# Near-lag matmuls in whole pieces in the odd chunk steps, prefix matmuls in the even ones

## The reference

```
xp = (X @ Wp + bp).reshape(B, T, 4, D)
f  = (pos @ Wf + bf).reshape(T, 3, D)          # pos: sines and cosines
y  = xp[:, :, 0]
for i in range(3):
    y = causal_conv(y, f[:, i]) * xp[:, :, i + 1]   # the reference does it by FFT
x = layernorm(x + y)
x = layernorm(x + (silu(x @ wg.T) * (x @ wu.T)) @ wd.T)
```

## Time and profile before

| | us |
|---|---|
| median of 3 runs | 971.78 (971.59 to 972.85) |
| the profiled execution | 972.62 |
| its span, first to last instruction | 970.4 |
| PE busy | 876.6 |
| DVE busy | 767.4 |
| POOL busy | 645.3 |
| ACT busy | 529.7 |

### The profile page before, as it was taken

The page is one execution under the profiler, slowest core; times in us unless marked ns, Lnnn a source line. Parts: engine busy times, 40 slices in busy tenths (PEclk is TensorE's granted clock), DMA queues, the critical chain, the costliest instruction groups (busy, mean ns, idle before and its releaser), DMA issues. The chain is left out here.

```text
span 970.4 us, 21584 instructions
## 1 busy us (share of the span) xinstructions
PE 876.6 (90%) x8204; PEld 678.0 (70%) x8204; DVE 767.4 (79%) x1318; ACT 529.7 (55%) x1048; POOL 645.3 (66%) x679
## 2 busy tenths in 40 slices
PE   3999999947999999999999999954899999999994
PEld 2888888846888888888888888732456556555563
DVE  2777777735899898888889889846688898988864
ACT  2253334446788888878887667314344444444441
POOL 2555555403888898898898889862676666667642
PEclk8999999969999999999999999996999999999998
DMA  5596556488566567566667877328123224222011
GB/s 205 192 348 214 188 173 205 165 230 238 164 189 174 165 194 197 174 179 175 193 195 213 262 235 209 109 105 276 45 66 120 77 65 130 65 77 74 23 45 44
DMA packets 165788, 155.16 MB, mean 160 GB/s; under 512 B 3457, under 2 KB 151937, under 8 KB 165313
## 3 DMA queue, kind: packets, MB, share of 16 engines
q1 hardware_dynamic: 164176, 145.24, 49.3%
q10 hardware_dynamic: 1520, 8.68, 2.3%
HBM read 111.18 MB, written 42.73 MB: 159 GB/s over the span
## 5 line engine op out<-in xcount | busy, mean ns | idle before, releaser
L564 POOL TENSOR_TENSOR gz<-prod 128x512 f32<-128x512 f32 x180 | 230.4, 1280 | 88.2 <-DVE prod L507 87.0
L507 DVE TENSOR_TENSOR prod<-bank,wfx 128x1024 f32<-128x1024 f32 x180 | 219.8, 1221 | 32.5 <-ACT bank L437 30.7
L396 PE MATMUL bank<-gz,ei 128*128 128x256 f32 x720 | 186.8, 382 | 2.2 <-POOL gz L564 2.0
L149 PE MATMUL bank<-wps,xs 128*128 128x512 f32 x768 | 176.4, 392 | 5.6 <-POOL xs L250 5.6
L149 PEld LDWEIGHTS bank<-wps,xs 128*128 128x128 f32 x768 | 145.6, 190 | 36.1 <-DVE wps L218 5.7
L939 POOL TENSOR_TENSOR hl<-hf,hh 128x512 f16<-128x512 f32 x96 | 111.8, 1173 | 82.4 <-ACT hh L793 82.4
L437 ACT COPY bank<-bank 128x512 f32<-128x512 f32 x180 | 102.8, 571 | 105.4 <-PE bank L344 105.4
L250 POOL TENSOR_TENSOR xs<-xt,xs 128x256 fp32r<-128x256 f32 x128 | 93.3, 752 | 97.4 <-ACT xs L181 97.4
L574 POOL TENSOR_TENSOR y<-y,gate 128x256 f32<-128x256 f32 x192 | 143.3, 747 | 5.1 <-DVE y L518 5.1
L344 PE MATMUL bank<-yh,ef 128*128 128x256 f16 x720 | 137.6, 273 | 2.3 <-ACT bank L437 1.3
L396 PEld LDWEIGHTS bank<-gz,ei 128*128 128x128 f32 x720 | 122.8, 190 | 15.8 <-POOL gz L564 6.5
(11 more groups left out here) (77 smaller groups left out, 1960.2 us busy)
## 6 DMA issues: line engine op xcount, KB each, us to landing
toep<-filter_rows SPq DMA_DIRECT2D x48, 1024.0 KB, 7.1
gates<-staged SPq DMA_DIRECT2D x16, 1536.0 KB, 6.3
gate<-gates SPq DMA_DIRECT2D x48, 512.0 KB, 4.1
xt<-in_XT SPq DMA_DIRECT2D x16, 512.0 KB, 5.0
attn_out<-y SPq DMA_DIRECT2D x16, 512.0 KB, 5.5
ya<-attn_out SPq DMA_DIRECT2D x16, 512.0 KB, 4.6
xr<-in_X SPq DMA_DIRECT2D x16, 512.0 KB, 5.4
out_x<-oo SPq DMA_DIRECT2D x16, 512.0 KB, 3.4
```

The source lines that it names most:

```text
L149: mm = pe.matmul(bank[n % 4 * 2 + half][:, :], xs[:, n % XSS, half, hx, k, :], wps[:, hw, k, half * 512:(half + 1) * 512], start=(k == 0 a ...
L396: mm = pe.matmul(dst, ei[:, h, e0 * P:(e0 + 1) * P], gz[:, n % 3, h, :], start=False, stop=(h == 1))
L507: nc.vector.tensor_tensor(prod[:, n % 2].rearrange("p r j (c b) -> p r j c b", b=NB), b_copy[n % 2][:, :].rearrange("p (r c b) -> p r c b" ...
L564: nc.gpsimd.tensor_tensor(gz[:, n % 3], prod[:, n % 2, 0], prod[:, n % 2, 1], ALU.add).then_inc(gz_ready, 1)
```

## The change

`toeplitz` is called for both parts of a piece in its odd step 2q+1; before, part 0 was in step 2q+1 and part 1 in step 2q+2, for the last piece in step 0 of the next pass. The prefix had 4 chunks (8 matmuls) in each of steps 3 to 14 (3 chunks in steps 6, 10 and 14); it now has 8 chunks (16 matmuls) in steps 4, 8 and 12 and 7 chunks (14 matmuls) in steps 6, 10 and 14. Step 15 keeps its 15 chunks. No matmul is added or removed, and nothing changes on the other engines.

```diff
                     for k in range(NA):
                         if 0 <= u < NU and k < NE:
                             state(u, k)
-                        if k == 0 and 0 <= u < NU:
-                            toeplitz(u, NQ - 1, 1)
                         if u + 1 < NU:
                             if k % 2:
                                 toeplitz(u + 1, k // 2, 0)
-                            elif k:
-                                toeplitz(u + 1, k // 2 - 1, 1)
+                                toeplitz(u + 1, k // 2, 1)
                             if k == 3 and u + 2 < NU:
                                 pe.wait_ge(norm_sum, u + 3)
                             if k == NA - 1:
                                 prefix(u + 1, 3, range(NE))
-                            elif k >= 3:
-                                prefix(u + 1, (k - 3) // 4, range((k - 3) % 4 * 4, min((k - 3) % 4 * 4 + 4, NE)))
+                            elif k % 2 == 0 and k >= 4:
+                                prefix(u + 1, (k - 4) // 4, range(0, 8) if k % 4 == 0 else range(8, NE))
```

## The result

The changed kernel takes 978.18 us (median of 6, 977.23 to 979.65) for 971.78 before. The ratio is 1.0066, with a 95% interval of 1.0053 to 1.0079: slower by more than 0.2%, in the direction forecast. It is 2.4 us above the predicted 975.8 and just outside the range given, 974.2 to 978.0. The profiled execution took 977.95 us for 972.62, 5.33 more.

A forecast was written before the change was run, and what follows sets the result against it. Passes were taken as bound by PE's steps 3 to 15 plus DVE's chain over the join; 11 x 0.36 = 3.96 us plus 0.10 in the first pass gave 4.06, median 975.8 us (+0.42%), range 974.2 to 978.0.

The forecast's parts named there:

- The ring of two links: Each pass: PE's work from step 3's near lags to step 15's readout, then DVE's gather(14) to low(1), some 6.6 us.
- the three places named: Steps 1, 2 and 3: PE's extra 0.36 us idle per join spread over waits for evacuate, pb and low(1).
- the 0.47 us put down to `norm`: Step 1: norm taken to need 0.47 us before the next state, putting state(2) 0.14 us later than before.
- the sum: Whole program: 3.96 us for 11 passes plus 0.10 for the first pass, 4.06 us slower.
- Is link A still without a wait?: PE from step 3's near lags to step 15's readout: 0 for new waits, bounds 0 and 6.6 us.
- alternating steps open new waits: Rival: 0.1 us in each even step of steps 4 to 14, or a late step 2 copy; 978 to 982, chance 0.07.
- the forecast's 0.36 us: Step 15: 12 near-lag matmuls of piece 7 moved in from step 0 of the next pass add 0.36 us per pass.
- its sign of being wrong: DVE's chain shortens, waits for copies, combine or evacuate appear in steps 4 to 14, or the 227.28 filter load shifts.
- The first pass: Pass u = -1, bound by a filter load until 227.28: +0.10 us, bounds -0.1 and +0.2 for the work behind it.
- No net cost: Rival: DVE's chain in the join shortens with PE's work, passes keep 34.83 us; about 971.9 us, chance 0.05.
- faster: Rival: pb starts ahead of POOL's combine, saving 0.78 us in each of 10 joins; about 967.6 us, chance 0.04.
- The gain in the first pass: Rival: half the first pass's time at the lower clock goes, -1.65 us; 974.2 us, chance 0.04.

The follow-up runs named there:

- run 1: Changed kernel with part 1 of piece 7 back in step 0 of the next pass: 973.49 us, ratio 1.0008 to the kernel before.
- run 3: Kernel before the change, with only part 1 of piece 7 moved from step 0 of the next pass to step 15: 976.65 us, ratio 1.0043.
- run 4: Kernel before the change, with all of piece 7 moved to step 0 of the next pass: 967.99 us, ratio 0.9943.
- run 7: Kernel before the change, PE order kept, with DVE's factors of a later unit moved behind low(1): 969.39 us, ratio 0.9964.
- run 2: Changed kernel with the prefix put ahead of piece 7 in step 15: 976.24 us, ratio 1.0039 to the kernel before.
- run 5: Changed kernel run again, unedited: 977.99 us, ratio 1.0063 to the kernel before.
- run 6: Changed kernel with the first pass (u = -1) in the halves and quarters of before, piece 7 whole in step 15: 978.12 us, ratio 1.0063.

## Why the prediction was right in kind and short in size

*The ring of two links* held. DVE's chain kept its length, DVE's wait before it grew by 0.35 us (1.86 for 1.51, predicted 1.87), and PE's idle time stands at the three places named: 0.2 us for `evacuate(7)`, 0.22 marked for `pb`, and the old 0.48 for `low(1)`. One term in this part was misread: the 0.47 us put down to `norm` held a wait of 0.25 for ACT's copy of step 1, which is why `state(2)` came 3.47 us after `state(0)` as before and not 0.14 later. It has no part in the sum. Runs 1, 3 and 4 put the price of the 12 matmuls at 0.35 to 0.38 us, and run 7 shows that DVE's chain is the other link.

*The step that failed* is the one headed "Is link A still without a wait?". I reckoned that the evacuation of an even step ends 2.2 us after the step's start and that the next near-lag matmul comes at 2.09 + 0.65 = 2.74. The 0.65 is the state of the odd step, and step 15 has none. There the matmul comes as soon as step 14 is over: 0.65 of state, 14 prefix matmuls and 0.98 of readout, 2.05 us. The 2.2 for the evacuation was right (369.88 - 367.70 = 2.18). Before, the step held 12 near-lag and 6 prefix matmuls, which take 0.13 us more, and the two came at the same time (run 3 has the old step 14 and waits 0.01 us there, 368.21 + 0.87 to 369.09): the 0.7 us to spare that the step gives for before was nothing here, and the 0.5 for after was a wait. It is 0.13 to 0.14 us (run 1's remainder, and the 0.14 that run 2 takes away), a term that the sum put at 0.

*The sum checked.* From the first `pv` to the last one, 11 passes later, it was 582.22 us before (231.76 to 613.98) and 587.59 in run 5 (230.02 to 617.61), and the same in run 6: 5.37 more, where the prediction has 3.96. Nine passes have 0.50 each, the first 0.49, and the last 0.38; that one's join holds no `factors`. The missing 1.4 us are in the main this wait. The 5.33 us of the first profiled pair agree with that by luck: there the 11 passes took 588.06 us, 5.84 more, 0.5 of it from the clock, and the rest of the program 0.5 us less. The bounds had 0 to 6.6 us for new waits, but I gave their rival 0.07 and let the range end at 978.0; the rival "alternating steps open new waits" was true in part, at one step of the pass instead of six and beside the forecast's 0.36 us. The prediction expected step 15 without a wait, while its sign of being wrong looked for new waits only in steps 4 to 14.

*The first pass*: I predicted +0.10 us. The profiled execution had +1.2, and the first `norm` came 1.2 us sooner (201.54 for 202.77), which cancels it there. Runs 5 to 7 show that the first pass varies by more than that with one and the same order, with the clock and with the filter load; the +0.10 can be neither confirmed nor refuted. Between the first timing (+6.4) and that of run 5 (+5.6) lies 0.8 us. The kernel before makes up 0.65 of it (971.78 and 972.43), the changed one 0.19; the runs tell no cause, and the two intervals overlap.

*The rivals.* "No net cost" is out by run 3, "faster" by `pb`, which kept its 1.21 us beside the `combine`. Its row for `pb` with POOL "at rest" was misread, for POOL's `combine` began 0.04 us behind `pb` there, and it was the `combine` that took longer, 1.51 us for 1.27:

```profile
234.31 1.51 POOL L564 TENSOR_TENSOR gz<-prod 128x512 f32<-128x512 f32 x1 [42.31 <-DVE prod L507]
```

So part of the 0.78 us could have come back on POOL. The gain in the first pass did not come (runs 5 and 6). The rule of the Trainium skill (Perfetto Trace Analysis, section Matmul Optimizations) that matmuls should come back to back in batches had nothing to add here: the granted clock of the block was 1.00 before and after.

## What to carry to other kernels

In a software-pipelined loop find out which engine sets the pace in which stretch, and price a moved instruction by the stretch it leaves and the one it enters; the same 12 matmuls cost 0.35 us a pass in one direction and gave 0.38 in the other, while total work stayed the same. When steps are made unequal, check every wait at the irregular steps of the loop, the first and the last above all, and not for a typical step. And look at starts, since a wait of 0.13 us that repeats 11 times carries no mark in the profile.

## What the runs showed of the hardware

The clock of TensorE fell to its lower level around the wait for a filter load in the first pass, in every profile, and it did not come back at a fixed distance from the resumed work. In the changed kernel it was back some 6 us after PE had gone on (226.34) in one execution and some 3.5 us after it (225.42) in the other. Between the two profiles that is a difference of 0.8 us from there to `pv` (5.41 for 4.60 us) and of 0.5 in the pass that follows (35.33 for 34.86), together nearly as much as the wait that the prediction had missed.

Of `pb` on DVE and the `combine` on POOL, the one that starts second takes longer. In the joins shown `pb` starts some 0.35 us into the `combine` and takes 1.20 to 1.21 us, the `combine` 1.27 to 1.28. In the second pass `pb` starts 0.04 to 0.05 us ahead and takes 0.41 to 0.42, and there the `combine` takes 1.50 to 1.51 us, in all 12 profiles. That `combine` is also POOL's first after some 42 us without one, and no run keeps the two apart.
